# A graph layer, attention over edges and four mixed experts on one core: where a row fix, a store, a mixing step and 27 scatters are placed

## The reference

```python
n  = layernorm(x)
x1 = x + relu(n @ W + segment_sum((n @ M)[src], dst))           # first layer
z  = layernorm(x1)
h  = (z @ W_gat)                                                 # 4 heads x 4 experts
e  = leaky_relu(a_src[src2] + a_dst[dst2])                       # 4 heads per edge
alpha = exp(e - segment_max(e)) / segment_sum(...)               # softmax per destination
agg = segment_sum(h[src2] * alpha) + b_gat
scores = mean over heads of layernorm(agg)                       # 4 expert scores per node
w  = softmax of the 2 best scores, 0 for the others
y_e = gelu(z @ W1[e] + b1[e]) @ W2[e] + b2[e]                    # all 4 experts, all nodes
out = x1 + sum_e w[e] * y_e
```

## Time and profile before

| | us |
|---|---|
| median of 3 runs | 3118.45 (3117.1 to 3118.94) |
| the profiled execution | 3111.18 |
| its span, first to last instruction | 3109.8 |
| PE busy | 2365.1 (76%) |
| DVE busy | 2271.1 (73%) |
| POOL busy | 2240.1 (72%) |
| ACT busy | 542.5 (17%) |

### The profile page before, as it was taken

One profiled execution on the slowest core, in us unless ns is written; L12 is line 12 of the kernel. 1 busy time (PEld: TensorE's weight loads), 2 busy tenths in 40 slices (PEclk: granted clock), 3 DMA queues, 4 the chain that ended last, 5 costly groups with the idle time before them and its releaser, 6 DMA issues. The chain is left out here.

```text
span 3109.8 us, 42414 instructions
## 1 busy us (share of the span) xinstructions
PE 2365.1 (76%) x13096; PEld 1848.5 (59%) x13096; DVE 2271.1 (73%) x6334; ACT 542.5 (17%) x924; POOL 2240.1 (72%) x2315
## 2 busy tenths in 40 slices
PE   1566787878879888879888989787899999988100
PEld 0344565556656555556666666565699988878100
DVE  6599877788887666566666656564479999989368
ACT  4000211211123333311111111111001110101012
POOL 3677777777777777777777777774777777777373
PEclk9787998989989998989999999998899999999555
DMA  8977777777767777768778777776212222221628
GB/s 273 327 221 223 226 224 216 231 227 226 242 203 244 243 233 239 237 208 267 244 233 254 234 251 246 251 245 190 60 44 63 67 67 65 63 63 33 204 59 267
DMA packets 470551, 599.71 MB, mean 193 GB/s; under 512 B 66293, under 2 KB 409270, under 8 KB 468278
## 3 DMA queue, kind: packets, MB, share of 16 engines
q1 hardware_dynamic: 372310, 375.12, 36.5%
q0 software_dynamic: 97568, 220.03, 25.6%
q10 hardware_dynamic: 448, 1.85, 0.2%
HBM read 312.22 MB, written 286.19 MB: 192 GB/s over the span
## 5 line engine op out<-in xcount | busy, mean ns | idle before, releaser
L1479 POOL DMA_INDIRECT ring<-xn_d,srci x1611 | 1573.7, 977 | 514.1 <-issue 453.0
L752 DVE SCALAR_TENSOR_TENSOR ring<-ring,same_v,wide 128x256 f32<-128x256 f32 x1610 | 770.3, 478 | 562.4 <-PE wide L1307 457.0
L1307 PE MATMUL wide<-ring,one_hot 128*128 128x256 f32 x3222 | 910.3, 417 | 284.5 <-DMA ring<-xn_d,srci 176.6
L1307 PEld LDWEIGHTS wide<-ring,one_hot 128*128 128x128 f32 x3222 | 636.6, 206 | 514.7 <-DMA ring<-xn_d,srci 197.8
L1409 PE MATMUL wide<-tab_parts,low_hot 128*128 128x208 bf16 x6144 | 574.2, 255 | 60.9 <-DVE low_hot L794 60.6
L1506 POOL DMA_INDIRECT g<-tab_d,srt x512 | 506.0, 988 | 156.0 <-issue 153.3
L1409 PEld LDWEIGHTS wide<-tab_parts,low_hot 128*128 128x128 bf16 x6144 | 552.5, 99 | 84.2 <-DVE low_hot L794 74.1
L1355 PE MATMUL wide<-xt,w1s 128*128 128x512 f32 (+1 forms) x832 | 389.5, 592 | 0.8 <-DVE feat L720 0.8
L1365 PE MATMUL wide<-w2s,hh 128*128 128x256 f32 x1568 | 384.0, 389 | 1.9 <-DVE yo L730 1.9
L689 DVE TENSOR_SCALAR one_hot<-iota_f,dloc 128x128 f32<-128x128 f32 x1611 | 363.3, 303 | 3.2
L1120 ACT ACTIVATE hh<-wide,b1c 128x512 f32<-128x512 f32 (+1 forms) x208 | 137.9, 663 | 1222.0 <-PE wide L1355 1221.7
(11 more groups left out here) (332 smaller groups left out, 1432.6 us busy)
## 6 DMA issues: line engine op xcount, KB each, us to landing
run_d<-ring SPq DMA_DIRECT2D x201, 1024.0 KB, 5.5
ring<-xn_d,srci POOLq DMA_INDIRECT x1611
y_d<-yo SPq DMA_DIRECT2D x196, 128.0 KB
comb<-y_d SPq DMA_DIRECT2D x28, 896.0 KB, 10.0
low_row<-low_d SPq DMA_DIRECT2D x16, 1024.0 KB
sum_d<-g SPq DMA_DIRECT2D x16, 768.0 KB, 3.5
g<-tab_d,srt POOLq DMA_INDIRECT x512
xn_d<-ring SPq DMA_DIRECT2D x7, 896.0 KB, 5.3
```

The source lines that it names most:

```text
L752: dve_at["run", j] = step(V.scalar_tensor_tensor(out=o, in0=ring[:, (j - 1) // JC % RING, (j - 1) % JC, :], scalar=same_v[:, j:j + 1], in1 ...
L1307: T.matmul(wide[:, 4 + j // 2 % 2, j % 2 * D:(j % 2 + 1) * D], one_hot[:, j // 4 % 4, j % 4, :], ring[:, j // JC % RING, j % JC, :], start ...
L1479: G.indirect_dma_start(out=ring[:, s, j % JC, :], out_offset=None, in_=xn_d, in_offset=at_rows(srci[:, j:j + 1])).then_inc(sem(f"gather{s} ...
```

## The change

- Row fix on chip. The corrected row of each partition is no longer scattered to `sum_d` and read back. It is spread by matmuls to the node and tile to which it belongs (`fix_r`), and `gate` masks the gathered sums by `keep` and adds `fix_r`. The gathers of `fsum` wait for nothing but the gather of the row.
- The last chunk's sums are stored ahead of the loads of the output stage.
- TensorE mixes 2 of the 7 tiles: ScalarE makes four diagonal matrices of expert weights, TensorE sums five matmuls (identity by `x1`, four diagonals by expert rows) in PSUM, ScalarE copies the sum back. GpSimd adds nothing.
- Four `comb` buffers instead of three; the fourth lies where edge data lay, so that its first load waits for these. A chunk's expert rows are loaded when the buffer's chunk is mixed, its `x1` rows when that chunk is stored.
- The destination scores of 27 of the 49 columns are scattered after the last gather of the first layer, before the wait for the last two tiles. They are read from `early`, a copy of the table made when tile 46 of 0 to 48 (in order of work) is stored. The two tiles that are missing in it (LATE = 2) are scattered from `feat2` after chunk 0's gathers, the other 22 columns behind them; each column's index leaves out the late tiles. The table is zeroed at the beginning (2 more stores).

```diff
-CR = 3
+CR = 4
-POOL_TILES = 2
+PE_TILES = 2
+DIAGS = 4
+LATE = 2
+EARLY_STARTS = 27
@@ sort_steps
+            for i in range(LATE):      # 4 small operations each on [P, 49]
...
@@ row fix (VectorE)
+        then(V.tensor_tensor(sm[:, 32:32 + FE], sm[:, 32:32 + FE], cfix[:, 0:FE], ALU.add))
+        step(V.tensor_scalar(node_of[:, :], iota_f[:, :], sm[:, 80:81], sm[:, 82:83], ALU.is_equal, ALU.mult))
+        then(V.tensor_scalar(tile_of, iota_f[:, 0:NT], sm[:, 81:82], None, ALU.is_equal))
+        dve_at["fix_rows"] = then(V.tensor_tensor(
+            fix_r[:, :, :], tile_of[:, :, None].broadcast_to([P, NT, FG]),
+            sm[:, None, 32:32 + FG].broadcast_to([P, NT, FG]), ALU.mult))
+        V.wait_ge(sem("rows_fixed"), 1)
+        then(V.tensor_scalar(keep, bank[3][:, 0:NT], -1.0, 1.0, ALU.mult, ALU.add))
+        step(V.tensor_tensor(keep, keep, has_f[:, :], ALU.mult))
+        for i, (a, b) in enumerate(FIX_PARTS):   # 21, 21 and 7 tiles
+            step(V.tensor_copy(fix_r[:, a:b, :], bank[4 + i][:, 0:(b - a) * FG]...))
@@ gate
-            then(V.tensor_tensor(fs, fs, hs.broadcast_to([P, n, FG]), ALU.mult))
+            then(V.tensor_tensor(fs, fs, smt[:, 1, t0:t1, None].broadcast_to([P, n, FG]), ALU.mult))
+            then(V.tensor_tensor(fs, fs, fix_r[:, t0:t1, :], ALU.add))
@@ ScalarE, per output chunk
+            for k in range(XG - PE_TILES, XG):
+                if mixed >= DIAGS:
+                    A.wait_ge(sem("mixed"), mixed - DIAGS + 1)
+                for e in range(NX):
+                    A.activation(diag[:, mixed % DIAGS, e, :], ident[:, :], ACT.Copy,
+                                 scale=fin[:, 7, c * XG + k, e:e + 1]).then_inc(sem("diags"), 1)
+                mixed += 1
+            for k in range(XG - PE_TILES, XG):
+                n = c * PE_TILES + k - (XG - PE_TILES)
+                A.wait_ge(sem("mixed"), n + 1)
+                A.activation(comb[:, s, NX, k, :], bank[4 + n % 4][:, 0:D], ACT.Copy).then_inc(sem("poured"), 1)
@@ TensorE
+        T.wait_ge(dve_step, dve_at["fix_rows"])
+        T.matmul(bank[3][:, 0:NT], tmask[:, :], smt[:, 0, :], start=True, stop=True)
+        for i, (a, b) in enumerate(FIX_PARTS):
+            mm = T.matmul(bank[4 + i][:, 0:(b - a) * FG], tmask[:, :], fix_r[:, a:b, :]..., start=True, stop=True)
+        mm.then_inc(sem("rows_fixed"), 1)
...
+                T.wait_ge(sem("diags"), NX * (n + 1))
+                T.matmul(bank[4 + n % 4][:, 0:D], ident[:, :], comb[:, s, NX, k, :], start=True, stop=False)
+                for e in range(NX):
+                    mm = T.matmul(bank[4 + n % 4][:, 0:D], diag[:, n % DIAGS, e, :], comb[:, s, e, k, :],
+                                  start=False, stop=(e == NX - 1))
+                mm.then_inc(sem("mixed"), 1)
@@ GpSimd
+        G.wait_ge(sem("early_in"), 16)
+        starts(range(EARLY_STARTS))
...
             if c == 0:
-                starts()
+                late_starts()
+                starts(range(EARLY_STARTS, NT))
...
-        G.wait_ge(dve_step, dve_at["fix_row"])
-        G.indirect_dma_start(out=sum_d, ..., in_=sm[:, 32:32 + FG], ...).then_inc(sem("fix_out"), 16)
-        G.wait_ge(sem("fix_out"), sent(0))
@@ SyncE
+                if k == NT - 1 - LATE:
+                    for i in range(2):
+                        Q.wait_ge(sem(f"tab_out{i}"), sent((k - i) // 2))
+                    Q.dma_start(early[:, :, :], tab_d.rearrange("(t p) f -> p t f", p=P)).then_inc(sem("early_in"), 16)
...
+        store_sums(NCF - 1)
         for c in range(CR):
-            load_comb(c)
-        store_sums(NCF - 1)
+            if c == CR - 1:
+                ...                     # waits: sums stored, carry done, exponentials done
+            for e in range(NX + 1):
+                load_rows(c, e)
         for c in range(NLN):
...
             if c + CR < NLN:
-                load_comb(c + CR)
+                for e in range(NX):
+                    load_rows(c + CR, e)
+            if 1 <= c <= NLN - CR:
+                Q.wait_ge(sem(f"out{(c - 1) % CR}"), sent((c - 1) // CR))
+                load_rows(c - 1 + CR, NX)
```

More of the change, by code:

```diff
@@ L167, in build @@
     idx_s = r.take("idx_s", [P, NT], I32)
+    late_i = r.take("late_i", [P, LATE], I32)
     has_f = r.take("has_f", [P, NT], F32)
@@ L213, in build @@
     q = Region(r4)
+    fix_r = q.take("fix_r", [P, NT, FG], F32)
+    q = Region(q.at - NT * HX * 4)
     fin = q.take("fin", [P, 8, NT, HX], F32)
+    hm = q.take("hm", [P, 2, HEADS, P], F32)
+    fsum = q.take("fsum", [P, NT, FG], F32)
     r.at = max(r.at, q.at)
@@ L261, in build @@
     comb = q.take("comb", [P, CR, NX + 1, XG, D], F32)
-    r.at = max(r.at, q.at)
-    hm = r.take("hm", [P, 2, HEADS, P], F32)
-    fsum = r.take("fsum", [P, NT, FG], F32)
+    diag = q.take("diag", [P, DIAGS, NX, P], F32)
+    early = r.take("early", [P, NT, FG], F32)
     oc = r.take("oc", [P, 9], F32)
@@ L303, in build @@
     PARTS = ((0, PART * XG), (PART * XG, NT))
-    ZERO_OUT = 16 * (FS + 1)
+    FIX_PARTS = tuple((a, min(a + 512 // FG, NT)) for a in range(0, NT, 512 // FG))
+    ZERO_OUT = 16 * (FS + 3)
     SHIFTED, SMALL, SCORES = 0, 64, 256
@@ L1034, in vector_program @@
             for e in range(NX):
-                for k in range(XG - POOL_TILES):
+                for k in range(XG - PE_TILES):
                     step(V.scalar_tensor_tensor(
@@ L1197, in gate @@
             A.wait_ge(dve_step, dve_at["gates", part])
+        mixed = 0
         for c in range(NLN):
@@ L1436, in tensor_program @@
         mm.then_inc(sem("carried"), 1)
+        T.wait_ge(dve_step, dve_at["fix_rows"])
+        T.matmul(bank[3][:, 0:NT], tmask[:, :], smt[:, 0, :], start=True, stop=True)
+        for i, (a, b) in enumerate(FIX_PARTS):
+            mm = T.matmul(bank[4 + i][:, 0:(b - a) * FG], tmask[:, :], fix_r[:, a:b, :].rearrange("p t f -> p (t f)"),
+                          start=True, stop=True)
+        mm.then_inc(sem("rows_fixed"), 1)
+        T.wait_ge(dve_step, dve_at["gates", 0])
+        for c in range(NLN):
+            s = c % CR
+            T.wait_ge(sem(f"comb_in{s}"), 16 * (NX + 1) * (c // CR + 1))
+            for k in range(XG - PE_TILES, XG):
+                n = c * PE_TILES + k - (XG - PE_TILES)
+                T.wait_ge(sem("diags"), NX * (n + 1))
+                if n >= 4:
+                    T.wait_ge(sem("poured"), n - 3)
+                T.matmul(bank[4 + n % 4][:, 0:D], ident[:, :], comb[:, s, NX, k, :], start=True, stop=False)
[3 more added lines that the diff above has]
+                mm.then_inc(sem("mixed"), 1)
     def gpsimd_program():
@@ L1480, in gpsimd_program, with starts, late_starts @@
                                      in_offset=at_rows(srci[:, j:j + 1])).then_inc(sem(f"gather{s}"), 16)
+        def starts(which):
+            for t in which:
+                G.indirect_dma_start(out=start_d, out_offset=at_rows(idx_s[:, t:t + 1]), in_=early[:, t, FE:FG],
+                                     in_offset=None, bounds_check=E2 - 1,
+                                     oob_is_err=False).then_inc(sem("start_out"), 16)
+        def late_starts():
+            for i in range(LATE):
+                k = NT - LATE + i
+                G.indirect_dma_start(out=start_d, out_offset=at_rows(late_i[:, i:i + 1]), in_=feat2[:, k % 2, FE:FG],
+                                     in_offset=None, bounds_check=E2 - 1,
+                                     oob_is_err=False).then_inc(sem("start_out"), 16)
+        G.wait_ge(sem("early_in"), 16)
+        G.wait_ge(sem("zero_out"), ZERO_OUT)
+        G.wait_ge(dve_step, dve_at["starts_at"])
+        starts(range(EARLY_STARTS))
         for s in range(RING):
@@ L1523, in gpsimd_program @@
                                      in_offset=at_rows(idx_f[:, t:t + 1])).then_inc(sem(f"node_in{part}"), 16)
[L1524 to L1536, removed]
     def sync_program():
@@ L1623, in sync_program @@
                 Q.dma_start(run_d[V_ * P:(V_ + 1) * P, :], zeros[:, 0:D]).then_inc(sem("zero_out"), 16)
+                table = tab_d.rearrange("(p a) f -> p (a f)", p=P)
+                Q.dma_start(table[:, 0:C2], zeros[:, :]).then_inc(sem("zero_out"), 16)
+                Q.dma_start(table[:, C2:NT * FG], zeros[:, 0:NT * FG - C2]).then_inc(sem("zero_out"), 16)
                 Q.wait_ge(sem("x_out"), 16 * NLN)
@@ L1728, in sync_program @@
             Q.wait_ge(dve_step, dve_at["combined", c])
-            Q.wait_ge(sem("added"), NX * POOL_TILES * (c + 1))
+            Q.wait_ge(sem("poured"), PE_TILES * (c + 1))
             n = min(XG, FULL // P - c * XG)
```

53 lines of the change are left out of this document (28 added, 25 removed).

## The result

The changed kernel takes 3042.23 us (median of 4 runs, 3039.66 to 3043.61) against 3118.69 (3117.1 to 3120.76): a ratio of 0.9754, with a 95% interval of 0.9737 to 0.977. It is faster. The forecast was 3041. Measured once more beside other kernels the two took 3042.05 and 3111.58, a ratio of 0.9781 (0.9768 to 0.9795): the kernel before differs by 7 us between the two measurements, the changed one by 0.2. So the sum is best judged in the profiled executions. Their spans are 3109.8 and 3038.4: 71.4 us, where the sum said 77.6.

What follows compares the result with a forecast made beforehand. GpSimd was taken to set the edge stage's end by a small lead, then a chain of waits the end stage. Summed terms ended the span at 3032.2 instead of 3109.8; 77.6 us off the median 3118.45 gave 3041, range 3033 to 3063.

Steps and rivals of the forecast that it cites:

- Row fix on chip: End stage: scatter, landing and waits of 7.14 us become one issue of 1.25; new fix work hidden with 15 us to spare.
- last `weigh`: End of the edge stage: weighing of the last chunk starts at 2880, 32.6 us earlier.
- row's gather to gate part 0: End stage: one issue, then 21 `fsum` gathers taking 27.3 us plus 3.6 under DMA load, ending at 2928.0.
- Gap: GpSimd's 36.8 us wait ending the first layer: 27 scatters take 34.7 us and fit; 1 us over was taken.
- the first `tab_d` gather not after 2185: Expected profile sign after the first layer: with the gap full of 27 scatters, this gather comes by 2185.
- SyncE's wait: Before the table copy: some 3 us extra, no store queued behind it before 2140, counted as nothing; 3 us if stalling.
- VectorE gives its waits back: Edge stage: without 13.2 us of waits for gathered columns, VectorE is ready for the last chunk at 2879.8 instead of 2893.0.
- Store first: End stage: last sums stored ahead of the loads, 3.9 us from store to the row's gather against 11.0 before.
- Mixing, TensorE, DMA: Output stage: 8.4 us a chunk, three chunks 25.3 and four 33.7; TensorE hidden at full clock; no chunk waits for DMA.
- Rival A: Mixing: TensorE stays at the low clock, 16 us more, 3057; chance 0.13.
- C: Gap: it doesn't hold the scatters, up to the whole 32 us lost, 3073; chance 0.04.
- D: End stage: `fsum` gathers starved by 18 MB of loads, slower than before, 3141 at 6 us each; chance 0.03.

Runs made afterwards that it cites:

- experiment 1: Changed kernel with EARLY_STARTS = 0, the gap left empty and all scatters after chunk 0's gathers: 3073.56 us, ratio 0.9877.
- experiment 8: Kernel before plus the two stores that zero the table: 3114.0 us; the same plus SyncE's wait and an unread copy of the table: 3115.03 us.
- Experiments 3 and 4: Changed kernel with the last sum store behind 15 loads: 3065.27 us; kernel before with only that store moved ahead of the loads: 3102.47 us.
- experiment 5: Changed kernel with the row fix through memory again, without fix matmuls or the gate's addition: 3050.07 us, ratio 0.9794.
- experiments 6 and 7: Changed kernel again: 3042.05 us; with three output buffers: 3050.83; with 18 tiles on TensorE instead of 14: 3033.8, repeated 3034.82; with 21: 3033.05.
- experiment 2: Changed kernel with the mixing of before: ScalarE scales, GpSimd adds, TensorE mixes nothing: 3064.7 us, ratio 0.9847.

## Why the prediction was right

Step by step, as the prediction put it, with its number and what the profile after has:

| step | predicted | measured |
|---|---|---|
| gap: `g` gathers begin later by | 1 | 6.1 (2188.8 for 2182.7) |
| VectorE ready for the last chunk | 2879.8 | 2880.6 (2884.17 - 3.57) |
| last `weigh` | 2880 | 2884.2 |
| sums ready to row's gather | 3.9 | 5.5 (2901.49 - 2896.00) |
| row's gather to gate part 0 | 32.2 | 32.3 |
| gate part 0 to mixing | 18.0 | 18.2 |
| three chunks | 25.3 | 25.2 |
| gate part 1 | 20.8 | 20.8 |
| four chunks | 33.7 | 33.6 |
| last VectorE operation to end | 6.4 | 6.7 |

Of the 6.2 us by which the span's gain fell short of the sum, 4.2 are in the last `weigh` and so in the gap, 1.6 in the store.

**Gap.** The scatters fit, but the term for the gap was mis-sized: 1 us was 6, and the sign that the prediction named, the first `tab_d` gather not after 2185, did not come. In the changed kernel's profile 3.7 us of it were there before the gap, at the last gather of the first layer (2147.4 for 2143.7), and 2.3 came in the gap.

The 3.7 us: in all ten profiles with the change the gap's beginning was late by 2.8 to 6.2 us. The prediction counted the first layer's stage as it is, because GpSimd issued "without a wait longer than 0.3 us". That holds for the stage's end only: over the whole stage GpSimd stood 13.2 us for the stores of its ring slots (7 times, up to 7.3 us) and up to 3.7 us at a time for VectorE in the kernel before, 16.0 (9 times, up to 9.0) and up to 3.9 in the changed one. Part of the lateness seems to go with the zeroed table: the 64th gather is issued at 152.2 and 152.5 in the two profiles without these stores, at 152.7 to 155.6 in the twelve with them. The rest stays open.

The 2.3 us: the row gather came at 2187.1 with the gap empty too (experiment 1), but there the gap began 2.5 us later, so this clears neither the scatters nor the copy. The traces point at the copy. In the eight profiles in which it is issued 4.3 to 6.1 us ahead of the last gather, TensorE stands 2.5 to 4.0 us for the last gathered rows, and from the last gather to tile 48's store it is 37.6 to 40.8 us. In the three in which it is issued 3.0 to 3.2 us ahead, and in the three without it, that wait is 1.1 us at most and the way 34.7 to 37.1. In seven of the eight TensorE's granted clock then fell to 0.50, and the matmuls that followed ran slower. One of the eight has the copy and no scatters (experiment 8), so the scatters aren't needed for it. No run moves the copy alone, so that this is the likely cause and not a shown one. The prediction took SyncE's wait as free; what it left out, if this holds, is what the copy does to the last gathers. All of it is at most 0.2% of the time.

**VectorE gives its waits back.** Right to 0.8 us. Since GpSimd was later than assumed, the last `weigh` hung on the gathers again and VectorE waited 3.6 us. Experiment 1 shows the other side: with 27 scatters more on GpSimd its waits go from 3.6 to 31.4 us.

**Store first.** The mechanism was right, the way took 5.5 us for 3.9. That the loads, issued 0.4 us behind the store, cause it is likely but not shown: no run has the last store without loads behind it. Experiments 3 and 4 show what the prediction had only in part: the store's place, the loads' beginning and the row fix's place depend on one another.

**Row fix on chip.** Hidden as computed, with 16 us to spare for 15. The prediction priced what it replaces at 7.1 us from a stretch in which DMA was nearly idle (3 GB/s from 2941 to 2948). With the loads beside it, it is 13.7 (experiment 5), so this part was worth twice what the sum of its own term shows. The sum didn't suffer: it was made for the new order as a whole.

**Mixing, TensorE, DMA.** Each term within 0.2 us. Rival A fell by the clock rows; A's price of 16 us was not tried. C and D didn't happen: the 27 scatters fit, and the `fsum` gathers came at 1.25 us with DMA at 337 GB/s (2900 to 2934).

**Parts and whole.** Undone one at a time the parts cost 32.7 (gap), 25.2 (GpSimd's adds), 20.9 (store), 13.0 (fix, with the 2.6 us ahead of it) by spans, and the fourth buffer 8.8 by medians: 100.6 together for a gain of 71.4. So the parts are not independent. For one pair the runs show it: to undo the store costs more in the changed kernel than it gains in the kernel before (20.9 for 8.3), and 7 us of the difference are the fix. That late chunks which wait for rows hide part of what slower mixing costs is argued from experiments 6 and 7, not run in pairs.

That the median came within 1.2 us of 3041 is partly luck: the spans were 6 us short of the sum, and the median of the kernel before was 7 us above its own profiled execution, and 5 to 7 above the medians of the four later measurements. The same 77.6 us taken off the profiled execution (3111.18) would have given 3033.6, where the changed kernel's took 3039.66.

## What to carry to other kernels

When a tail is a chain of small steps, write the chain out in absolute times for the new order, and price each DMA round trip by the load that will then be on the queues, not by the load that the old profile had: here a row fix of 7 us became 14. An engine that adds a small share of elementwise work can cost another engine as much as it takes off it: here 3.6 us a chunk for the 3.4 that the two tiles would take VectorE itself (8 x 0.42, an estimate). TensorE, which took the same share, cost VectorE nothing. And the idle time at a stage change is a place for work that later stands in a queue that sets the end, as long as what it reads can be had early.

## What the runs showed of the hardware

VectorE's fused multiply-adds on 256 floats per partition took 0.42 us each without and 0.87 beside GpSimd's additions (5 in 2.08 and in 4.33 us) in the kernel before, and 5 in 2.08 and in 4.3 in experiment 2. A gather of 128 rows of 96 bytes was seen 2.4 us after its issue with DMA free, 5.6 to 8.7 with the output loads at 320 to 350 GB/s beside it, but GpSimd's rate of issue, 1.25 us, was not touched. TensorE's granted clock stayed at 1.00 through the mixing's idle stretches of 1.7 us and was 0.50 behind those of 27 and 38 us. Behind the single waits for the last gathered rows it was mixed: 1.00 after 2.74 us in the changed kernel's first profile, and down to 0.50 after 2.98 us in its second.
